# Centring the output weights once, and pairing the output transposes and projections, in a sandwich of linear attention and mixture of experts

## What is computed

```python
def _layernorm(x, axis=-1, eps=1e-05):
    m = jnp.mean(x, axis=axis, keepdims=True)
    v = jnp.var(x, axis=axis, keepdims=True)
    return (x - m) / jnp.sqrt(v + eps)

# attention: 8 heads of 32, causal linear attention by chunks of 64, with a running state
o = chunked_linear_attn(q, k, v)
z = jnp.cumsum(k, axis=1)
denom = jnp.maximum(jnp.abs(jnp.sum(q * z, axis=-1)), DENOM_EPS)[..., None]
o = rmsnorm(o / denom, norm_w)
attn = jnp.einsum('bse,de->bsd', o.reshape(b, s, H * D), Wo)

# experts: 8, all computed, 256 inner
h = jax.nn.silu(gate) * up
out = jnp.einsum('bte,betd->btd', weights, jnp.einsum('beti,eid->betd', h, Wd))

x = x + _layernorm(attn(_layernorm(x)))
x = x + _layernorm(ffn(_layernorm(x)))
```

## Time and profile before

| | |
|---|---|
| median of 3 runs | 1507.49 us (1507.42 to 1509.41) |
| the profiled execution | 1508.8 us |
| its span, first to last instruction | 1507.1 us |
| TensorE busy | 1468.6 us, 97% |
| VectorE busy | 997.0 us, 66% |
| ScalarE busy | 680.4 us, 45% |
| GpSimd busy | 453.7 us, 30% |
| mean granted TensorE clock | 0.994 of 2.4 GHz |

### The profile page before, as it was taken

One profiled execution on the slowest core, in us unless ns is written; L12 is line 12 of the kernel. 1 busy time (PEld: TensorE's weight loads), 2 busy tenths in 40 slices (PEclk: granted clock), 3 DMA queues, 4 the chain that ended last, 5 costly groups with the idle time before them and its releaser, 6 DMA issues. The chain is left out here.

```text
span 1507.1 us, 37448 instructions
## 1 busy us (share of the span) xinstructions
PE 1468.6 (97%) x14436; PEld 1280.9 (85%) x14436; DVE 997.0 (66%) x2388; ACT 680.4 (45%) x1261; POOL 453.7 (30%) x720
## 2 busy tenths in 40 slices
PE   7799999999999999999999999999999999999997
PEld 6678888888888888888888888888888888888886
DVE  4646766666676766766666676766766666776765
ACT  4543544445344453545445344453535445344433
POOL 1422512234141332512234141332513234141231
PEclk9999999999999999999999999999999999999999
DMA  3300000000000000000000000000000000000000
GB/s 113 112 1 2 21 7 14 14 14 14 0 14 14 14 14 0 21 7 14 14 14 14 0 14 14 14 14 0 25 3 14 14 14 14 0 14 16 2 8 22
DMA packets 25345, 24.59 MB, mean 16 GB/s; under 512 B 2016, under 2 KB 25056, under 8 KB 25312
## 3 DMA queue, kind: packets, MB, share of 16 engines
q1 hardware_dynamic: 25312, 24.13, 5.0%
HBM read 15.74 MB, written 8.39 MB: 16 GB/s over the span
## 5 line engine op out<-in xcount | busy, mean ns | idle before, releaser
L677 ACT ACTIVATE h_hi<-late 128x512 fp32r<-128x512 f32 x256 | 161.6, 631 | 271.7 <-DVE late L956 271.5
L956 DVE TENSOR_TENSOR late<-late,up_ps 128x512 f32<-128x512 f32 x256 | 175.4, 685 | 158.0 <-PE up_ps L422 100.6
L422 PE MATMUL down_ps<-w_hi,h_hi 128*128 128x256 f32 x976 | 264.5, 293 | 0.0
L422 PE MATMUL down_ps<-w_hi,h_lo 128*128 128x256 f32 x976 | 253.9, 282 | 0.0
L758 ACT ACTIVATE late<-gate_ps 128x512 f32<-128x512 f32 x256 | 151.9, 593 | 220.9 <-PE gate_ps L422 216.3
L1164 POOL TENSOR_TENSOR rms_in<-rms_in,minus_half 128x16 f32<-128x16 f32 x32 | 93.8, 2930 | 510.7 <-DVE rms_in L920 510.7
L978 DVE SCALAR_TENSOR_TENSOR late<-down_ps,route,late 128x256 f32<-128x256 f32 x364 | 158.6, 477 | 105.6 <-PE down_ps L422 102.7
L871 DVE TENSOR_TENSOR h_lo<-late,h_hi 128x512 fp32r<-128x512 f32 x256 | 175.5, 685 | 64.7 <-ACT h_hi L677 64.7
L422 PE MATMUL gate_ps<-ft_hi,w_hi 128*128 128x512 f32 x512 | 204.3, 399 | 0.7 <-ACT ft_hi L677 0.4
L422 PE MATMUL gate_ps<-ft_hi,w_lo 128*128 128x512 f32 x512 | 203.0, 397 | 0.0
L422 PE MATMUL up_ps<-ft_hi,w_hi 128*128 128x512 f32 x512 | 199.3, 389 | 0.0
(11 more groups left out here) (161 smaller groups left out, 2571.6 us busy)
## 6 DMA issues: line engine op xcount, KB each, us to landing
xs<-in_x SPq DMA_DIRECT2D x32, 256.0 KB, 2.9
out_rows<-late SPq DMA_DIRECT2D x32, 256.0 KB, 2.2
late<-in_wg SPq DMA_DIRECT2D x8, 256.0 KB, 3.3
late<-in_wu SPq DMA_DIRECT2D x8, 256.0 KB, 2.7
late<-in_wd SPq DMA_DIRECT2D x8, 256.0 KB, 3.0
late<-in_wkv_t SPq DMA_DIRECT2D x1, 512.0 KB, 5.4
late<-in_wq_t SPq DMA_DIRECT2D x1, 256.0 KB, 4.6
late<-in_wo_t SPq DMA_DIRECT2D x1, 256.0 KB, 4.7
```

The lines of the kernel that those rows point to most:

```text
L422: last = nc.tensor.matmul(dst, lhs, rhs, start=n == 0, stop=n == len(terms + low_terms) - 1)
L677: return nc.scalar.activation(dst, src, ACT.Copy)
L956: nc.vector.tensor_tensor(h_f[:, m, :], h_f[:, m, :], up_ps[m][:, :], ALU.mult).then_inc(h_ready[0], 1)
```

## The change

- The output weights are centred once: after the scaling with `norm_w`, VectorE takes the mean of each row of `wo_raw` over the 256 outputs and subtracts it. The projected rows then have mean zero.
- ScalarE's copy of the projected rows and its `ln2_apply` are gone. VectorE takes the statistics of the projected rows in PSUM, GpSimd makes only the inverse root (`root_only`, two instructions), and VectorE multiplies by it and adds the residual in one instruction for each tile, again from PSUM. The PSUM banks of `wo` are free once `x1` is written.
- Of the 28 slots, the two output transposes stand in one (18) and the two projections in one (20), with a pair of buffers for the transposed output. `ln2_stats` of both halves, `ln2_add` 0 and `ln3_stats` 0 stand in slot 21, `ln2_add` 1 in 22, `ln3_stats` 1 in 23.
- The first block has an order of its own for each engine. Its input, its first norm, its projection `q` and its transposes go by halves of the tokens; the first and third norm are applied by VectorE; `wkv` is loaded ahead of `wq`; the units of weights come through eight buffers (two in `x1`) and stand one by one in the orders. The steps that follow the first up-projection wait for fewer units.

```diff
 STEPS = [
...
     [("norm_apply", 0)],
-    [("ot", 0)],
+    [],
     [("norm_apply", 1), ("carry",)],
-    [("wo", 0), ("ot", 1)],
-    [("ln2_stats", 0)],
-    [("wo", 1), ("ln2_apply", 0)],
-    [("ln2_stats", 1), ("ln2_add", 0), ("ln3_stats", 0)],
+    [("ot", 0), ("ot", 1)],
     [],
-    [("ln2_apply", 1), ("ln2_add", 1), ("ln3_stats", 1)],
+    [("wo", 0), ("wo", 1)],
+    [("ln2_stats", 0), ("ln2_stats", 1), ("ln2_add", 0), ("ln3_stats", 0)],
+    [("ln2_add", 1)],
+    [("ln3_stats", 1)],
     [("ln3_apply", 0)],
...
+FIRST_PE = [("xt", 0), ("kv", 0), ("q", 0), ("xt", 1), ("su", 0), ("kv", 1), ("kt", 0), ("kt", 1), ("s", 0), ("q", 1), ("su", 1),
+            ("o", 0), ("s", 1), ("o", 1), ("ot", 0), ("wo", 0), ("ot", 1), ("wo", 1), ("ft", 0), ("ft", 1)]
...
+FIRST_DVE = [("x_stats", 0), ("x_norm", 0), ("low", "wkv"), ("xt", 0), ("x_stats", 1), ("scale", "wo"), ("low", "wq"),
...
             READ_OUT["ot", p] = (ot_ready, p + 1)
-            READ_OUT["wo", p] = (wo_copied, p + 1)
+            READ_OUT["wo", p] = (x1_ready, p + 1)
...
                 elif kind == "ln2_stats":
                     p = step[1]
-                    reach(dve, wo_copied, a, p + 1)
-                    ln_stats(2, rows, range(2 * p, 2 * p + 2), bn2, mv2)
+                    reach(dve, att_done, a, number_of(("wo", p), a) + 1)
+                    for b in range(B):
+                        last = nc.vector.bn_stats(bn2[:, 2 * p + b, :], att_half(("wo", p), a)[:, b, :])
+                    settle(last)
+                    for t in range(2 * p, 2 * p + 2):
+                        last = nc.vector.bn_aggr(mv2[:, t, :], bn2[:, t, :])
+                    last.then_inc(moments_ready[1][0], 1)
                 elif kind == "ln2_add":
                     p = step[1]
-                    ts = slice(2 * p, 2 * p + 2)
-                    reach(dve, ln2_applied, a, p + 1)
+                    reach(dve, rstd_ready[1], a, p + 1)
                     reach(dve, x1_copied, a, 0)
-                    nc.vector.tensor_tensor(x1[:, ts, :], rows[:, ts, :], xs[:, ts, :], ALU.add).then_inc(x1_ready[0], 1)
+
+                    for b in range(B):
+                        t = 2 * p + b
+                        last = nc.vector.scalar_tensor_tensor(x1[:, t, :], att_half(("wo", p), a)[:, b, :], rstd2[:, t:t + 1],
+                                                              xs[:, t, :], ALU.mult, ALU.add)
+                    last.then_inc(x1_ready[0], 1)
...
+                    for g in range(HG):
+                        last = nc.vector.bn_stats(bn4[:, g, :], wo_raw[:, g, :])
+                    settle(last)
+                    for g in range(HG):
+                        last = nc.vector.bn_aggr(mv4[:, g, :], bn4[:, g, :])
+                    settle(last)
+                    for g in range(HG):
+                        last = nc.vector.tensor_scalar(wo_raw[:, g, :], wo_raw[:, g, :], mv4[:, g, 0:1], None, ALU.subtract)
+                    last.then_inc(wo_scaled, 1)
...
+            def root_only(n, p, a, mv, var, rstd):
+                ts = slice(2 * p, 2 * p + 2)
+                reach(pool, moments_ready[n - 1], a, p + 1)
+                settle(nc.gpsimd.tensor_tensor(var[:, ts], mv[:, ts, 1], ln_eps[:, ts], ALU.add))
+                nc.gpsimd.tensor_tensor(rstd[:, ts], var[:, ts], minus_half[:, 0, ts], ALU.pow).then_inc(rstd_ready[n - 1][0], 1)
```

More of the change, by code:

```diff
@@ L319, in att_half, with is_first @@
             columns = {"q": 512, "kv": 512, "s": 512, "su": B * HG * PAIR, "o": B * HPG * VA}.get(step[0], 256)
-            return att_ps[:, 2 * n, :] if step[0] == "q" else att_ps[:, 2 * n:2 * n + 2, 0:columns]
+            if step[0] == "q" and not is_first(a):
+                return att_ps[:, 2 * n, :]
+            return att_ps[:, 2 * n:2 * n + 2, 0:256 if is_first(a) and step[0] == "q" else columns]
+        def is_first(a):
+            return psum_order(a) is FIRST_PSUM_STEPS
         def prob_of(p, a):
-            return probs[0 if psum_order(a) is FIRST_PSUM_STEPS else p]
+            return probs[1 - p if is_first(a) else p]
         def is_last(f):
@@ L695, in att_step @@
                 kind = step[0]
-                if step in PSUM_STEPS and kind not in ("s", "su", "ft"):
+                if step in PSUM_STEPS and kind not in ("s", "su", "wo", "ft"):
                     reach(act, att_done, a, number_of(step, a) + 1)
                     src = att_half(step, a)
+                half = slice(2 * P * step[1], 2 * P * step[1] + 2 * P) if len(step) > 1 else None
                 if kind == "xt":
-                    copy(halves(xt_hi[:, step[1], :]), src).then_inc(xt_hi_ready[0], 1)
+                    copy(xt_hi[:, :, half] if is_first(a) else halves(xt_hi[:, step[1], :]), src).then_inc(xt_hi_ready[0], 1)
                 elif kind == "q":
-                    copy(q_t[:, step[1], :], src).then_inc(q_ready[0], 1)
+                    copy(q_t[:, :, half] if is_first(a) else q_t[:, step[1], :], src).then_inc(q_ready[0], 1)
                 elif kind == "kv":
@@ L722, in att_step @@
                 elif kind == "ot":
-                    copy(ot_hi, src).then_inc(ot_hi_ready[0], 1)
-                elif kind == "wo":
-                    p = step[1]
-                    copy(rows[:, 2 * p:2 * p + 2, :], src)\
-                        .then_inc(wo_copied[0], 1)
+                    copy(ot_hi[step[1]], src).then_inc(ot_hi_ready[0], 1)
                 elif kind == "ft_out":
@@ L733, in att_step @@
                         .then_inc(ft_hi_ready[0], 1)
-                elif kind == "ln2_apply":
-                    p = step[1]
-                    ln_apply(2, p + 1, a, rows, rows, range(2 * p, 2 * p + 2), shift2, rstd2).then_inc(ln2_applied[0], 1)
                 elif kind == "ln3_apply":
@@ L889, in att_step @@
                     k = step[1]
+                    half = slice(2 * P * k, 2 * P * k + 2 * P)
+                    lo, hi = (xt[:, :, half] if is_first(a) else halves(xt[:, k, :]) for xt in (xt_lo, xt_hi))
                     reach(dve, xt_hi_ready, a, k + 1)
-                    low(halves(xt_lo[:, k, :]), att_half(step, a), halves(xt_hi[:, k, :])).then_inc(xt_ready[0], 1)
+                    low(lo, att_half(step, a), hi).then_inc(xt_ready[0], 1)
                 elif kind == "s":
@@ L1129, in settle, with inverse_root @@
                 pool.wait_ge(pool_own, 1).then_inc(pool_own, -1)
-            def inverse_root(n, k, tiles, a, mv, var, rstd, shift):
+            def inverse_root(n, k, tiles, a, mv, var, rstd, shift, count=1):
                 reach(pool, moments_ready[n - 1], a, k)
@@ L1210, in _ @@
             nc.gpsimd.tensor_tensor(odd_even[:, :], diag[:, 0:2, 0], diag[:, 2:4, 0], ALU.add).then_inc(const_ready, 1)
-            x_root((0, 0))
-            for steps in FIRST_STEPS:
-                for step in steps:
-                    att_step(step, (0, 0))
+            for step in FIRST_POOL:
+                att_step(step, (0, 0))
             x_root((1, 0))
```

284 lines of the change are left out of this document (156 added, 128 removed).

## The result

The changed kernel takes 1530.18 us (median of 4 runs: 1529.71, 1530.66, 1531.74 and 1524.96) against 1507.48 us for the kernel before on the same chip: 1.0141 times as long, 95% interval 1.0116 to 1.0167. The profiled execution took 1529.71 us, its span is 1528.0; before, 1508.8 and 1507.1. So the two spans differ by 20.9 us.

The account below looks back on a forecast made before the run. TensorE, busy 90% or more in 37 of 40 slices, was taken as the bound. 1508.8 - 14.5 (first block) + 24 (stalls) + 7 (clock) = 1525.3, less 1.3 for the median: 1524 us, range 1500 to 1543 (0.82).

Parts of the forecast that it names:

- the side that had 0.76: Whole kernel: the chance given to the changed kernel being slower than before.
- The stall: Steady blocks: down(6,0) waits for VectorE's low part, a new 2.1 us in each of 15 blocks; net +24 us.
- The soft link: VectorE's slot 21 in steady blocks: a wait of about 0.25 us for GpSimd's root before the first add.
- What `ft` gives back: Steady blocks: the transposes' wait on ScalarE's third-norm copies goes, giving back 0.56 us a block.
- The clock: Steady blocks: stalls let TensorE's clock fall, four falls taken, +7 us; ends 0 and 25.5 us.
- PSUM as a source: VectorE's statistics read from PSUM: no extra cost charged; the skill's rule would add 3.9 us.
- The first block: First block's new order: shorter chain saves 14.5 us, ends -9 and -18.
- The head: First block up to `kv 0`: starts near 11.7 instead of 14.94, -3.3 us; `q 0` then waits some 1.7 us.
- The middle: First block, `kv 0` to second output projection: 33.9 us instead of 37.9, -4.0; ends -1 and -6.
- The tail: First block, second output projection to first up-projection: about 9.5 us instead of 16.7, -7.2; ends -5 and -8.
- No stall: Rival for steady blocks: VectorE still delivers before 876.5, 8.4 and 14.5 us both won, 1484 us; chance 0.14.
- The stall without falls: Rival for steady blocks: the stall comes but the clock does not fall, 1517 us; chance 0.24.

Follow-up runs that it names:

- the first experiment: Changed kernel with only TensorE's two output projections put back in separate slots, 19 and 20, other engines' steps left in place: 1531.39 us.
- the doubled statistics: Changed kernel with the second half's statistics taken twice in slot 21 of the loop: 1541.94 us.
- The filled gap: Changed kernel with seven matmuls without use on TensorE in front of down(6,0): 1522.70 us.
- the spread: Changed kernel with projections in slots 19 and 20, first half's statistics in slot 20, second add in slot 23: 1500.78 us.
- the early table: Changed kernel with both projections and their statistics in slot 19, first add in 20, second add and first third-norm statistics in 21: 1491.77 us.
- the last experiment: VectorE's steps early plus idle matmuls in the first block; there, copies and roundings for the second key/value projection moved ahead of the output weights: 1490.98 us.

## Why the prediction came out right, and where its terms were off

The result, 1530.18, lies in the range of 1500 to 1543, 6 us above the forecast of 1524, on the side that had 0.76. Step by step:

- **The stall.** Predicted 2.1 us in each block with its walk on VectorE, measured 2.0. From the start of `add_down(5, 0)` to the end of the low part the walk gave 869.91 to 878.58, 8.67; the trace has 600.93 to 609.54, 8.61. The soft link, the wait for GpSimd's root, came out at 0.2 for 0.25. Net of the wait for `ft`: predicted 1.6 (92 as the period), measured 1.55. That agreement is a little too good: the prediction has the restart twice, once in 878.7 and once as the 0.1 that it adds, and without that it says 1.5 a block, 23 us. That it sits in VectorE's order and not in the paired projections is shown by the first experiment, and the one-to-one price by the doubled statistics.
- **What `ft` gives back.** Predicted 0.56; the period of 89.75 without any stall shows 0.55. It is not additive with the stall, though: with the stall halved it came back, so taking away 0.8 us of the stall was worth only 0.15 a block.
- **The clock.** Predicted four falls of 1.7 us, found four of 1.55; that it was just four is luck, since the ends were 0 and 15. The filled gap shows that they cost time (7.5 us by the medians) and that the gap causes them. Gaps of 1.07 us gave 0 of 15, of 1.85 4 of 15, twice, and of 2.52 5 of 15. The changed kernel's own runs lie 6.8 us apart, and four falls are 6.2. Its fastest run, 1524.96, has a mean granted clock of 0.994, the others 0.991 and 0.992; but no profile of that run exists, so where in it the clock fell is not shown. The Trainium skill, page "TensorE: Matmul & The Clock Gate", Part 1, has activity release the full clock; matmuls without use in the gap held it at 1.00 here, which agrees.
- **PSUM as a source.** Charged nothing. Changed kernel by line (mean ns behind the bar):

```profile
L898 DVE BATCH_NORM_STATS2 bn<-x 128x6 f32<-128x256 f32 x64 | 24.0, 416 | 0.6
L968 DVE BATCH_NORM_STATS2 bn<-att_ps 128x6 f32<-128x256 f32 x64 | 23.9, 415 | 0.6 <-PE att_ps L434 0.6
```

  Statistics from SBUF take 416 ns and from PSUM 415. The 65 ns an instruction estimated from the Trainium skill, page "VectorE: DVE Perf Modes", section on the TRN2 errata, are not there, so its 3.9 us are not in the sum.
- **The first block: the step that failed.** Predicted -14.5, measured -9.0. The head was right: `kv 0` at 11.65 for 11.7, and `q 0` waits 1.45 on Wq's low part for 1.7. To the digit it is luck, since in the runs with this same first block `kv 0` came between 11.04 and 12.30. The middle was predicted at 33.9 and took 36.7 (11.65 to 48.38), a gain of 1.2 for 4.0. One of its links I can name: the second output projection waits 1.07 until the first's PSUM bank is free, which now is only when VectorE has written `x1`, since the copy is gone (the diff's line in `READ_OUT`, which my walk left out). Two pauses of TensorE that the profile gives no releaser (0.65 at 32.95 and one of 0.32) are another 1.0 in the sum, but no loss against the kernel before, whose middle has 1.3 of them (0.15 and the row below, from its timeline). The other 1.7 or so lies spread over some thirty links, and stays open.

```profile
37.84 0.46 PE L428 MATMUL att_ps<-state,q_t 64*64 64x66 f32 x16 [1.18 <-issue]
```

  The tail took 10.6 for 9.5, with waits of 1.10 and 1.30 for VectorE's third-norm rows ahead of the two `ft` steps. The term that was too small is GpSimd's root, put at 1.2 both times: from the end of the statistics to the next step of VectorE it took 1.5 (51.27 to 52.81) and 1.8 (54.87 to 56.68). In the first an addition took 0.55 us where it takes 0.20 elsewhere, in the second the power took 1.25 for 0.70, and both times VectorE was making the low part of a weight unit meanwhile. Both are as long in the traces of the spread and of the early table. That the two engines hinder each other there is not tested. The changed kernel:

```profile
55.40 1.25 POOL L1199 TENSOR_TENSOR rstd<-var,minus_half 128x2 f32<-128x2 f32 x1 [0.18 <-POOLq L1184]
55.40 0.68 DVE L893 TENSOR_TENSOR w_lo<-late,w_hi 128x512 fp32r<-128x512 f32 x1
...
56.68 0.74 DVE L912 TENSOR_SCALAR rows<-x,mv,rstd 128x256 f32<-128x256 f32 x2 [0.59 <-POOL rstd L1199]
```

  And "from the up-projection to the wait that ends at 79.03 nothing changes" missed 1.6, a fall of the clock behind the up-projection. It is not certain from run to run: with the same waits of 1.1 and 1.3 ahead of it, two of the seven traces with this order (spread steps, doubled work) have no fall in the first block. 3.3 + 1.2 + 6.1 - 1.6 = 9.0.
- **The sum** was 1508.8 - 14.5 + 24 + 7; it is 1508.8 - 9.0 + 23.3 + 6.2 = 1529.3, against 1529.71 for the profiled execution. The first block was 5.5 us dearer than forecast, the other two terms 1.5 cheaper.
- **The rivals.** No stall (1484) did not come; it describes the table with VectorE's steps early, 1491.8, which is 1484 with the first block's shortfall of 5.5 and 2 more. The stall without falls (1517) is the filled gap, 1522.7, again with that shortfall. The first up-projection was forecast near 55 and came at 58.97, still under the 60 that I had named as the mark of error; in the seven traces with this first block it came between 57.68 and 60.67, once over the mark.

## What to carry to other kernels

When an engine that is 66% busy gets late for one that never stops, its busy share says nothing: find the instruction of the other engine that it must wait for, and count its work from there to the deadline. Work that does not depend on that event belongs ahead of it; here the same steps, put one and two slots earlier, turned 22.7 us of loss into 15.7 of gain. And when a copy is dropped, ask what it had set free: the PSUM bank now lives until the last reader.

## What was not expected

- A gap's price in clock is uneven: after 1.85 us of idle time TensorE fell back in 4 of 15 blocks that are alike in the timeline, and in the repeat in other blocks (from 140, 330, 790 and 1250 us; then 150, 420, 880 and 1340).
- The start of the first projection moves from run to run: the same 28 warming matmuls at the start took 4.79 to 6.26 us, and `kv 0` came between 10.90 and 12.38. Differences of about 1 us between kernels need the distance from `kv 0`, not the time from zero.
- TensorE paused up to 1.59 us within one group of small matmuls with no releaser in the profile. The traces point to the loading of its instructions. In eight traces (the changed kernel and seven experiments) the pause stands ahead of the same instruction, the 10th of the 64 matmuls, and a second one, where there is one, 256 recorded TensorE instructions later. The profile's instruction queue q8 moves 16 KB at a time, and the long pause ends 1.3 to 1.5 us after the end of such a transfer (31.41 and 32.95 in the changed kernel, 32.22 and 33.72 in the last experiment), the second 1.2 to 1.5 us after the next one's. No run varied this, so it is a reading and not shown, and the pauses at other places (0.22 to 0.76 ahead of a group of 16) are not explained by it.
